# Keys and values of an attention stage as three products of rounded halves, in a decoder layer on one core

## The reference

```
x = _layernorm(x + attn(x, ...))                     # mixer
x = _layernorm(x + xattn(x, ctx, ctx, Wq, bq, Wk, bk, Wv, bv, Wo, bo))
x = _layernorm(x + ffn(x, Wr, W1, W2))               # experts

# in xattn:
q = query @ Wq.T + bq
k = key @ Wk.T + bk          # key = value = ctx, 256 x 256 a sequence
v = value @ Wv.T + bv        # 16 heads of 16
scores = einsum(q, k) / sqrt(16); attn = softmax(scores)
out = einsum(attn, v) @ Wo.T + bo
```

## Time and profile before

| | |
|---|---|
| median of 3 runs | 884.67 us (882.44, 884.67, 884.70) |
| profiled execution, its own time | 883.86 us |
| span of the profile, first to last instruction | 882.0 us |
| mean granted clock of TensorE | 0.959 of its full speed |
| busy share of PE, PE weight loads, DVE, ACT, POOL | 90%, 71%, 68%, 46%, 40% |
| loop step of `attend` (start of the values to the next) | 26.7 and 27.0 us in turn |

### The profile page before, as it was taken

The page is one execution under the profiler, slowest core; times in us unless marked ns, Lnnn a source line. Parts: engine busy times, 40 slices in busy tenths (PEclk is TensorE's granted clock), DMA queues, the critical chain, the costliest instruction groups (busy, mean ns, idle before and its releaser), DMA issues. The chain is left out here.

```text
span 882.0 us, 16600 instructions
## 1 busy us (share of the span) xinstructions
PE 798.2 (90%) x5754; PEld 628.3 (71%) x5754; DVE 595.9 (68%) x1456; ACT 402.6 (46%) x644; POOL 353.5 (40%) x292
## 2 busy tenths in 40 slices
PE   8998987788999999999999998776799999999995
PEld 6776765555766666666666676544799999999994
DVE  5889873456777777777877768655356666666654
ACT  5665652135545655456555455453343234323420
POOL 1332353322445444455454544224421553255335
PEclk9999999689999999999999999898799999999999
DMA  4111922444445435354444443230503422342201
GB/s 133 49 35 60 286 81 76 139 123 144 124 142 174 126 112 162 127 170 144 120 143 145 136 156 109 85 119 33 178 21 106 139 87 83 134 148 86 87 3 49
DMA packets 76081, 100.93 MB, mean 114 GB/s; under 512 B 11065, under 2 KB 63522, under 8 KB 76024
## 3 DMA queue, kind: packets, MB, share of 16 engines
q1 hardware_dynamic: 72568, 92.06, 34.6%
q0 software_dynamic: 3456, 8.13, 2.6%
HBM read 65.47 MB, written 35.74 MB: 115 GB/s over the span
## 5 line engine op out<-in xcount | busy, mean ns | idle before, releaser
L1301 DVE TENSOR_REDUCE nmax<-ps_m 128x4 f32<-128x1024 f32 x128 | 156.6, 1223 | 56.8 <-PE ps_m L881 46.9
L1099 ACT ACTIVATE pt<-ps_a 128x1024 f32<-128x1024 f32 x128 | 131.4, 1027 | 99.8 <-PE ps_a L891 75.9
L1574 ACT ACTIVATE hid<-ps_h 128x640 fp32r<-128x640 f32 x64 | 45.1, 705 | 147.1 <-PE ps_h L1502 147.1
L1502 PE MATMUL ps_h<-xt,w_hi 128*128 128x320 f32 x512 | 101.5, 321 | 1.0 <-DVE xt L1589 1.0
L881 PE MATMUL ps_m<-kst,qst 48*128 48x256 f32 x512 | 67.1, 341 | 29.7 <-DVE nmax L1301 23.7
L881 PEld LDWEIGHTS ps_m<-kst,qst 48*128 48x128 f32 x512 | 40.2, 193 | 66.1 <-DVE nmax L1301 33.4
L1684 POOL DMA_INDIRECT out_rows<-gated,token x40 | 50.1, 1253 | 91.5 <-issue 91.5
L1639 DVE SCALAR_TENSOR_TENSOR hid<-ps_h,hid 128x640 fp32r<-128x640 f32 x64 | 52.8, 824 | 49.3 <-ACT hid L1574 48.9
L1502 PEld LDWEIGHTS ps_h<-xt,w_hi 128*128 128x128 f32 x512 | 80.6, 192 | 4.1 <-DVE hid L1639 2.5
L757 POOL TENSOR_TENSOR half<-kq,half 128x512 fp32r<-128x512 f32 x32 | 41.6, 1301 | 102.0 <-ACT half L1065 102.0
L1516 PE MATMUL ps_y<-w,hid 128*128 128x512 f32 x320 | 80.3, 393 | 0.7 <-DVE gated L1657 0.7
(11 more groups left out here) (211 smaller groups left out, 1605.3 us busy)
## 6 DMA issues: line engine op xcount, KB each, us to landing
halves_dram<-half SPq DMA_DIRECT2D x64, 256.0 KB, 2.5
gated<-in_w SPq DMA_DIRECT2D x16, 1024.0 KB, 5.1
kst<-halves_dram SPq DMA_DIRECT2D x64, 128.0 KB, 2.6
qst<-halves_dram SPq DMA_DIRECT2D x64, 128.0 KB, 2.8
rows_dram<-blank SPq DMA_DIRECT2D x1, 5160.0 KB, 20.5
gated<-rows_dram SPq DMA_DIRECT2D x7, 645.0 KB, 4.2
x_raw<-in_x_t SPq DMA_DIRECT2D x8, 512.0 KB, 3.9
xres<-in_x SPq DMA_DIRECT2D x16, 256.0 KB, 3.3
```

The lines of the kernel that those rows point to most:

```text
L1099: nc.scalar.activation(pt[:, k % 4].rearrange("p s t q -> p (s t q)"), ps_a[:].rearrange("p s t q -> p (s t q)"), ACT.Exp).then_inc(s["exp ...
L1301: nc.vector.tensor_reduce(nmax[:, q, :, :, h // 2].rearrange("p t s -> p s t"), ps_m[:], AX.X, ALU.max, negate=True).then_inc(s["max_done" ...
L1502: mm = pe.matmul(ps_h[:, f % 2, c2, 0:HC], w1[a][:, p, k, f * P:(f + 1) * P], xt[:, b, p, k, c2 * HC:(c2 + 1) * HC], start=(n == 0 and k = ...
L1574: nc.scalar.activation(hid[:, HI, f, :].rearrange("p (c n) -> p c n", c=2), ps_h[:, f % 2, :, 0:HC], ACT.Relu).then_inc(s["hid_hi"], 1)
```

## The change

The context and the two weights are split into halves, and keys and values become three products each. The halves of the weights and of the first batch's context are made at the end of `mixer_in`. In each step of `attend` the high half of the next batch's context is made by ScalarE at slot 11, and the low half by VectorE at slot 13. TensorE's keys wait for the low half instead of for the load. The load of the context waits for the low half of two batches ago instead of for keys and values. To make room, the new weights' tile lies where the raw weights of the mixer were, and one semaphore of `experts` is replaced by one of the first part.

```
@@ mixer_in, ScalarE, last group of tokens
+                if g == NG - 1 and m < 3:
+                    act.wait_ge(c["loaded"], 16 * len(c["loads"]))
+                    if m < 2:
+                        nc.scalar.copy(c["w_kv2"][:, m, 0], c["w"]["kv"[m]][:]).then_inc(c["ctx_hi"], 1)
+                    else:
+                        act.wait_ge(s["ctx_in0"], 16)
+                        nc.scalar.copy(c["ctx2"][:, 0, 0], c["ctx"][:, 0]).then_inc(c["ctx_hi"], 1)
@@ mixer_in, VectorE
+                if (g, m) == (NG - 1, 3):
+                    for i, n in enumerate("kv"):
+                        dve.wait_ge(c["ctx_hi"], i + 1)
+                        nc.vector.tensor_tensor(c["w_kv2"][:, i, 1], c["w"][n][:], c["w_kv2"][:, i, 0].bitcast(F32),
+                                                ALU.subtract).then_inc(c["ctx_lo"], 1)
+                    dve.wait_ge(c["ctx_hi"], 3)
+                    nc.vector.tensor_tensor(c["ctx2"][:, 1, 0], c["ctx"][:, 0], c["ctx2"][:, 0, 0].bitcast(F32),
+                                            ALU.subtract).then_inc(c["ctx_lo"], 1)
@@ attend
+    PARTS = ((0, 0), (0, 1), (1, 0))
@@ attend, SP: load_ctx
-            need(sp, s["k_mm"], j - 1)
-            need(sp, s["v_mm"], j - 1)
+            need(sp, c["ctx_lo"], j + 1)
@@ attend, TensorE: keys
-                pe.wait_ge(ctx_in[p], use(j, 16, p))
+                pe.wait_ge(c["ctx_lo"], j + 3)
                 pe.wait_ge(s["r1_done"], j + 1)
-            for k in range(KD):
-                mm = pe.matmul(ps_d[:, m * S:(m + 1) * S], w["k"][:, k, m * P:(m + 1) * P], ctx[:, p, k, :],
-                               start=(k == 0), stop=(k == KD - 1), skip_group_check=True)
+            for n, (a, b) in enumerate(PARTS):
+                for k in range(KD):
+                    mm = pe.matmul(ps_d[:, m * S:(m + 1) * S], c["w_kv2"][:, 0, a, k, m * P:(m + 1) * P], ctx2[:, b, p, k, :],
+                                   start=(n == 0 and k == 0), stop=(n == 2 and k == KD - 1), skip_group_check=True)
@@ attend, TensorE: values
-            for k in range(KD):
-                mm = pe.matmul(ps_d[:, t * D:(t + 1) * D], ctx[:, p, k, t * P:(t + 1) * P], w["v"][:, k, :],
-                               start=(k == 0), stop=(k == KD - 1), skip_group_check=True)
+            for n, (a, b) in enumerate(PARTS):
+                for k in range(KD):
+                    mm = pe.matmul(ps_d[:, t * D:(t + 1) * D], ctx2[:, b, p, k, t * P:(t + 1) * P], c["w_kv2"][:, 1, a, k, :],
+                                   start=(n == 0 and k == 0), stop=(n == 2 and k == KD - 1), skip_group_check=True)
@@ attend, ScalarE, ahead of the exponentials of slot 12
+                if h == 11 and on(n, -1) and not (isinstance(n, int) and n < 0):
+                    act.wait_ge(ctx_in[q], use(n + 1, 16, q))
+                    need(act, s["v_mm"], n)
+                    nc.scalar.copy(ctx2[:, 0, q], ctx[:, q]).then_inc(c["ctx_hi"], 1)
@@ attend, VectorE, slot 13
                 if h == 13 and on(n, -1) and not first:
+                    dve.wait_ge(c["ctx_hi"], n + 4)
+                    nc.vector.tensor_tensor(ctx2[:, 1, q], ctx[:, q], ctx2[:, 0, q].bitcast(F32), ALU.subtract
+                                            ).then_inc(c["ctx_lo"], 1)
                     dve.wait_ge(s["wout_mm"], n + 2)
                     dve.wait_ge(s["x_added"], n + 2)
@@ experts, SP and GpSimd (all five places)
-                sp.wait_ge(s["setup3"], 1)
+                sp.wait_ge(c["blank_ready"], 3)
@@ decoder
+                with nc.sbuf_tensor("w_raw", [P, KD, 2, MH, P], F32) as early:
+                    c["w_raw"] = early
+                c["w_kv2"] = hold("w_kv2", [P, 2, 2, KD, D], F32R)
```

More of the change, by code:

```diff
@@ L77, in mixer_in @@
     PARTS = ((HI, HI), (HI, LO), (LO, HI))
-    w_raw = T("w_raw", [P, KD, 2, MH, P], F32)
+    w_raw = c["w_raw"]
     w_in = [T("w_in_hi", [P, KD, 2, MH, P], F32R), T("w_in_lo", [P, KD, 2, MH, P], F32R)]
@@ L566, in attend @@
     xres, ctx, sb, y, r1, x1, st1, mv1, ve1, power = (c[n] for n in "xres ctx sb y r1 x1 st1 mv1 ve1 power".split())
+    ctx2 = c["ctx2"]
+    PARTS = ((0, 0), (0, 1), (1, 0))
     st2, mv2, ve2 = T("st2", [P, KT, 6], F32), T("mv2", [P, KT, 2], F32), T("ve2", [P, KT], F32)
@@ L1424, in experts @@
     names = """rows_in0 rows_in1 turn_mm turn_hi turn_lo hid_mm hid_hi hid_lo w1_hi w1_lo w2_hi w2_lo out_mm res_part res_done
-        var_ready rstd new_done sent0 sent1 step3 token_done setup3 stats_done""".split()
+        var_ready rstd new_done sent0 sent1 step3 token_done stats_done""".split()
     s = {n: sem("e_" + n) for n in names}
@@ L1672, in _ @@
     def _(pool):
-        nc.gpsimd.memset(power[:], -0.5).then_inc(s["setup3"], 1)
-        pool.wait_ge(s["setup3"], 1)
+        nc.gpsimd.memset(power[:], -0.5).then_inc(c["blank_ready"], 1)
+        pool.wait_ge(c["blank_ready"], 3)
         def w2_lo(e, p):
@@ L1761, in decoder @@
                 for n, shape, dt in (("bq", [P, KD], F32), ("tri_b", [P, P], BF16), ("ones_b", [P, P], BF16),
-                                     ("ones_r", [NH * S // P, P], F32R)):
+                                     ("ones_r", [NH * S // P, P], F32R), ("ctx2", [P, 2, 2, KD, S], F32R)):
                     c[n] = hold(n, shape, dt)
-                for n in ("loaded", "blank_ready", "rows_blank", "scan_out", "scaled", "st_mm", "st_ready"):
+                for n in ("loaded", "blank_ready", "rows_blank", "scan_out", "scaled", "st_mm", "st_ready", "ctx_hi", "ctx_lo"):
                     c[n] = sem(n)
```

## The result

The kernel with the change takes 886.64 us (median of 20 runs, 883.92 to 890.60), the kernel before, in the same rounds, 882.40 us (20 runs, 878.79 to 884.75). The ratio is 1.0046 with a 95% interval of 1.0032 to 1.0060: some 4.1 us slower. The profiled execution took 886.74 us (span 884.9), with a mean granted clock of 0.952.

A forecast was written before the change was run, and what follows sets the result against it. A closed path through values, scores, `dest`, sends, `x2b`, `r`, statistics and maxima was taken to bound each step. Terms +0.3 (11 steps), +1.5 (first), -0.8 (last) made +1.0 on 883.86: 885 us, range 880 to 891.

The forecast's parts named there:

- likeliest case: Attention steps: the subtraction eats what the values gain, so the time stays the same; 883 to 888.5 us, chance 0.50.
- Values, -0.39 us a step: TensorE, each attention step: twelve rounded products take 1.44 us instead of 1.83, a gain of 0.39 us on the path.
- Keys worth nothing: TensorE, each attention step: 0.20 us gained twice goes into waits for the maxima, which become 0.78 and 0.57 us.
- Cast and load, 3.3 us to landing: ScalarE, each step: load lands 3.3 us after issue, exponentials run late, the projection some 0.5 us; 0.78 us spare covers it.
- Subtraction, +0.42: VectorE, each step: the subtraction collides with GpSimd's additions for `x2b`, so `r` comes 0.42 us later.
- The rival that it is hidden: Attention steps: subtraction and GpSimd's addition overlap freely, a step gains 0.39 us, 880.4 us in all; chance 0.20.
- Sum of a loop step, +0.03: One attention step: -0.39 for the values and +0.42 for the subtraction; over 11 steps +0.3 us.
- First steps, +1.5: Second and third loaded batch: load to `r` needs 4.7 us, `r` is 0.95 and 1.32 us late, less 0.39 each.
- First step, "ahead of which nothing is loaded": Very first attention step: left out of the 11 steps that were charged +0.03 us each.
- End of the mixer, 0: End of the first stage: three casts and three subtractions (2.1 us) hide in existing waits; 2.1 us without that cover.
- Last steps, -0.8: Last two batches of values: no cast beside them, so -0.39 us twice.
- Clock, 0.23 for 890.5: Rival: longer TensorE waits make its clock fall, about 1.4 us each; four falls in 11 steps give 890.5 us; chance 0.23.

The follow-up runs named there:

- products_only: The changed kernel without cast and subtraction in the steps, halves of the first context standing in for every batch: 876.74 us, ratio 0.9937 to the kernel before.
- early_both: The changed kernel with the context load issued at the start of the step and the subtraction moved to slot 11, ahead of the maxima: 886.18 us, ratio 1.0046.
- early_load: The changed kernel with only the context load moved to the start of the step: 885.83 us, ratio 1.0038 to the kernel before.
- early_keys_full: early_both with the keys left as full float32 products, only the values as three products: 879.16 us, ratio 0.9952 to the kernel before.
- filler_keys: early_both with four spare products a step ahead of the first half of the keys: 875.59 us, ratio 0.9900 to the kernel before.
- after_filler: The changed kernel with four spare products a step, load and subtraction where the change has them: 882.72 us, ratio 0.9993 to the kernel before.

## Why the prediction was right or wrong, point by point

The number was near (885.0 for 886.64, inside the range), but my likeliest case was no change within 0.3%, and it is 0.46% slower. The loop came out as summed; what is ahead of it did not.

*Values, -0.39 us a step:* right in the total, which is 0.38 in products_only, but in part by luck. The twelve products took 1.60 us and not 1.44, so by themselves they gain 0.23. From the transposes ahead of them to the scores behind them (433.12 to 435.13 in products_only, 434.78 to 437.09 in before_again) it is 0.30; the last 0.08 is spread over the step.

*Keys worth nothing:* right for the path (loop steps with full and with short keys are equal, twice). The waits for the maxima behind them were to be 0.78 and 0.57 us; in the loop they are 0.81 and lower in the change's two profiles, and 0.96 or more in early_both and early_load. What I didn't see is that shorter keys can cost clock: with the load early they did (early_both against early_keys_full). I had counted the lengthened wait only as a risk.

*Cast and load, 3.3 us to landing:* right in size (3.03 to 4.16 us, 14 loads), but I said that 0.78 us covered the late exponentials. By my own numbers (442.12 to 444.6) these were 2.5 us late, not 2; from the scores behind the values to them it is 6.93 us in the step shown (441.46 to 448.39) against 3.84 before, 3.1 more. In 6 of the last 9 steps of the profile TensorE waits 0.2 to 1.1 us for them (0.53 in the step shown), mostly in place of a wait for the maxima behind it; so it costs little there.

*Subtraction, +0.42:* right, with its mechanism: `r` starts 0.47 us after `x2b` in the step shown (449.17 to 449.64) where it started 0.11 us after, so it is 0.36 us later. The rival that it is hidden is out: early_load shows the wait on both sides.

*Sum of a loop step, +0.03:* measured -0.03 (26.81 against 26.84 on average). Right.

*First steps, +1.5:* right in what it counts: from load to `r` 0.96 and 1.12 us more (4.72 against 3.76, 4.51 against 3.39) where I had 0.95 and 1.32, less the values. I left out the step ahead of these two: there `r` waited for TensorE as well (0.69 us, at 180.12) and came 3.96 us after the issue of its load, less than the 4.7 us that I counted; now it is 4.29. From the first `r` to the fifth it is 2.0 to 2.8 us in all (104.14 and 104.35 in the change's two profiles, 102.16 and 101.53 in those of the kernel before). Of its two stretches, the clock is lower in both pairs of profiles only from 210 to 235 (0.93 against 1.00). With the load early it is 102.44, 99.86 and 100.45 us (early_both, early_load, early_keys_full).

*First step, "ahead of which nothing is loaded":* wrong. The halves of the second batch are made there too. The subtraction stood behind GpSimd's own subtraction for the low half of the queries (153.02 to 154.29) and took 1.34 us instead of 0.69; then the first addition of `x2b` stood behind it and took 1.73 us instead of 1.27 (the earlier trace rows has the pattern): `r` was some 0.5 us later.

*End of the mixer, 0:* right for VectorE, whose wait of 2.97 us shrank to 0.27. But behind it the first queries took 3.46 us instead of 1.99, at half the clock in part; not foreseen, and its cause is open. From the mixer's last add to the first `r` it is 22.53 and 22.69 us in the change's two profiles, 20.61 and 21.66 in those of the kernel before.

*Last steps, -0.8:* not to be told from the clock's scatter.

*Clock, 0.23 for 890.5:* the mechanism is shown where the load is early (early_both against early_keys_full and filler_keys). In the change its place was another than I said: the loop steps of both profiles have no fall, the stretches ahead of them do. The likeliest case had 0 for it; some 2.4 us by the executions' clocks is an estimate.

*The term that was mis-sized* is what stands ahead of the loop. From the mixer's last add to the fifth `r` the sum had +1.5 us (0 for the end of the mixer and the very first step, +1.5 for two late steps), and both pairs of profiles show 3.9 us more (126.67 against 122.77, 127.04 against 123.19). Moving the load alone takes 3 us of it away in early_load's profile, so the late load is most of it.

What was only argued: how these 3 us divide between waiting for the load and the lower clock. They overlap, since a late load leaves TensorE waiting in the first steps as well. Open are the fall at the first queries and where after_filler's executions gain.

## What to carry to other kernels

When a new operation stands between a load and its use, look at the steps in which that load has the least time: the loop hid most of the late load here, the first steps did not. And before shortening work on an engine, ask whether it fills a wait. With the load early, TensorE's shorter keys bought a longer wait, and the lower clock that followed cost more than the products had (886.18 us against 879.16 with full keys); without the casts and subtractions the same keys cost no clock (products_only). The change with the load issued at the start of the step, the subtraction away from GpSimd's additions and the keys left alone is 0.5% faster than the kernel before; with the shorter keys and spare products in the wait it is 1.0% faster, of which the spare products alone give some 0.3% to the kernel before. Look at the granted clock of every timed execution, not only at one profile's.

## What the runs showed of the hardware

A scattered send of GpSimd took 1.33 us instead of 1.09 where VectorE's subtraction of two SBUF tiles ran beside it (early_both: 443.87 to 445.20, the subtraction 443.55 to 444.23); this is the 0.24 us by which its steps without a fall stay longer than those of products_only. And more work made the kernel faster: 64 spare products (four in 0.67 us in the step shown, 418.26 to 418.93) took 10.6 us off the time of early_both.
